# Causal attention scores from fp32 operands in 32-partition groups, two heads at a time

## The reference

```
q, k, v = (layernorm(x) Wq + bq), (ctx Wk + bk), (ctx Wv + bv)   # 4 batches x 16 heads of 16
QEr  = q . Er^T                                # (b, h, 512, 512)
Srel = skew(QEr)                               # row i shifted by its distance to the diagonal
attn = softmax(causal((q k^T + Srel) / 4)) v
x    = x + attn
x    = x + moe_ffn(layernorm(x));  x = x + cross_attention(layernorm(x));  x = x + ternary_ffn(x)
```

## Time and profile before

| | us |
|---|---|
| median of three runs | 1235.87 (1233.3 to 1241.53) |
| the profiled execution | 1240.44 |
| its span | 1238.3 |
| opening, up to the first `relative` | 0 to 86.6 |
| causal attention, to its last DVE instruction | 86.6 to 394.2 |

### The profile page before, as it was taken

How to read it: one execution, slowest core, us unless ns; L and a number is a source line. 1 busy time by engine, 2 the same in 40 slices (tenths; PEclk the granted TensorE clock), 3 DMA queues, 4 the chain that set the end, 5 groups by cost and what they waited for, 6 DMA issues and landing times. The chain is left out here.

```text
span 1238.3 us, 22330 instructions
## 1 busy us (share of the span) xinstructions
PE 1011.7 (82%) x6466; PEld 632.3 (51%) x6467; DVE 698.7 (56%) x2148; ACT 649.7 (52%) x1354; POOL 199.1 (16%) x466
## 2 busy tenths in 40 slices
PE   5746778877888769899999993538999999987487
PEld 3413455444454559898899993212333333334344
DVE  3844778888887541121111110866766666683697
ACT  1345767777773423222233331425777777763687
POOL 0000000000000012233222210002222222240232
PEclk9876999999999979899999997668999999998699
DMA  7478989999983845666666662463111111110001
GB/s 234 149 261 317 332 326 341 342 341 339 339 335 108 315 136 202 220 212 216 215 216 228 221 218 77 131 207 106 46 46 46 48 45 45 46 31 9 1 30 39
DMA packets 91721, 220.29 MB, mean 178 GB/s; under 512 B 8854, under 2 KB 52214, under 8 KB 85654
## 3 DMA queue, kind: packets, MB, share of 16 engines
q1 hardware_dynamic: 87926, 209.46, 49.2%
q0 software_dynamic: 3744, 10.23, 2.2%
HBM read 143.14 MB, written 76.41 MB: 177 GB/s over the span
## 5 line engine op out<-in xcount | busy, mean ns | idle before, releaser
L775 DVE CUSTOM_DVE_ANT_0 unused<-mpsS,mask_bias 128x512 bf16<-128x512 f32 x256 | 172.0, 691 | 84.0 <-PE mpsS L708 83.8
L1482 ACT ACTIVATE hT<-ph,w 128x128 f32<-128x128 f32 x312 | 89.0, 368 | 208.8 <-PE ph L1456 208.8
L802 ACT ACTIVATE mPT<-mpsB 128x512 f32<-128x512 f32 x256 | 152.6, 597 | 81.2 <-PE mpsB L715 74.8
L1456 PE MATMUL ph<-xT,w 128*128 128x128 f32 x1248 | 151.5, 281 | 8.8 <-DMA w<-in_w1p 8.1
L1501 DVE TENSOR_TENSOR xn<-py,b 128x256 f32<-128x256 f32 x39 | 16.5, 424 | 248.7 <-PE py L1466 248.7
L555 PE MATMUL psT<-ident,scores 128*128 128x128 f32 x640 | 108.0, 285 | 57.2 <-ACT scores L648 55.3
L1456 PEld LDWEIGHTS ph<-xT,w 128*128 128x128 f32 x1248 | 146.9, 197 | 11.9 <-issue 10.9
L603 DVE CUSTOM_DVE_ANT_0 scores<-psS,bias 128x512 f32<-128x512 f32 (+3 forms) x256 | 119.7, 487 | 47.8 <-DMA bias<-rel 21.8
L643 ACT COPY stage<-psE 128x512 f32<-128x512 f32 (+1 forms) x192 | 97.5, 510 | 93.6 <-DMA rel<-stage 58.1
L1466 PE MATMUL py<-w,hT 128*128 x624 | 141.2, 379 | 0.7 <-DVE xn L1501 0.7
L648 ACT ACTIVATE scores<-scores,nm 128x128 f32<-128x128 f32 (+3 forms) x256 | 136.6, 565 | 5.2 <-DVE nm L616 5.2
(11 more groups left out here) (258 smaller groups left out, 1435.8 us busy)
## 6 DMA issues: line engine op xcount, KB each, us to landing
rel<-stage SPq DMA_DIRECT2D x64, 640.0 KB, 6.6
bias<-rel SPq DMA_DIRECT2D x64, 640.0 KB, 7.2
w<-in_w1p SPq DMA_DIRECT2D x39, 1028.0 KB, 5.7
qk<-packed SPq DMA_DIRECT2D x64, 192.0 KB
mqk<-packed SPq DMA_DIRECT2D x64, 192.0 KB
w<-in_w2p SPq DMA_DIRECT2D x8, 1024.0 KB
b<-in_b SPq DMA_DIRECT2D x39, 128.0 KB, 6.1
got<-pair_out SPq DMA_DIRECT2D x8, 512.0 KB, 8.3
```

The costliest lines, as they stand in the source:

```text
L775: nc.vector.tensor_tensor_reduce(out=unused[:, i, :], in0=psS[i % 2][:, :], in1=mask_bias[:, i, :], scale=1.0, scalar=-3.0e38, op0=ALU.add ...
L802: nc.scalar.activation(PT[r][:, j, :], psB[j % 2][:, :], ACT.Exp, scale=1.0 / 4).then_inc(s_exp, 1)
L1456: mm = nc.tensor.matmul(ph[half][:, q * P:(q + 1) * P], w1[i][:, dk * F + f * P:dk * F + (f + 1) * P], xT[i][:, dk, :], start=(dk == 0), s ...
```

## The change

- `packed`, `qk`, `ErP` and the splitting go out of the first attention. Queries (`qf`, in the memory of `xn`) and keys (`kf`, in that of `xnT`) stay in SBUF as fp32, with `er` repeated over the partitions. The weights' rows are reordered on the host so that heads m of eight lie in four groups of 32 partitions: head m in group m mod 4, in its lower 16 partitions for m mod 8 < 4, in its upper 16 for the others. For an upper head the query comes from a copy in which the lower 16 rows are zeroed (`odd`), and all 32 rows are contracted.
- Heads go in pairs. `psE`, `psS`, `psT` are one pair of banks each, a bank for each head; ACT's stage copy, DVE's `PT` copy and the scaling of the maxima treat both heads in one instruction. One transfer of 1.28 MB writes `stage` for the pair, one reads `bias`.
- The stages are `REL` 5, `READ` 4, `SOFT` 2, `EXP` 1, now in pairs; there is no `LOAD`. PE's order in a unit is score of both heads, relative of both heads, the mask of both, then the transposes. All is written out, without the loop.
- `bias` has a third buffer in x's memory and zeroed queries are in ctxT's, so x and ctxT are read again at the end of the block.
- In the opening, LayerNorm goes batch by batch behind the values; ACT makes one copy of each product.

```
-            LOAD, REL, READ, SOFT, EXP = 8, 6, 4, 2, 1
+            REL, READ, SOFT, EXP = 5, 4, 2, 1
...
-                psE = banks(ctx, "psE", 2)
+                psE = ctx.enter_context(nc.psum_tensor("psE", [P, 2, 512], F32))   # psS, psT likewise
...
+                def where(p, h):
+                    m = 2 * p + h
+                    b, eh, odd, r = m // HEADS, m % HEADS // ROUND, m % ROUND // GROUP, m % GROUP
+                    return b, eh, odd, slice(ROWS * r, ROWS * r + (ROWS if odd else DH))
...
+                    def read(p):
+                        sp.wait_ge(s_wr[slot], 16 * (p // RING + 1))
+                        if p >= len(bias):
+                            sp.wait_ge(s_soft, 2 * NU * (p - len(bias) + 1))
+                        skewed = bass.AP(rel[slot].ap().tensor, P - 1, [[2 * REL_W - 1, P], [1, 2 * REL_W]])
...
+                    for n in range(-REL, NP - SOFT):
+                        if (p := pair_at(n, READ)) is not None:
+                            read(p)
+                        if (p := pair_at(n, REL)) is not None:
+                            write(p)
...
+                    def relative(p, u):
+                        wait(pe, s_eev, NU * p + u)
+                        for h in range(2):
+                            rows = where(p, h)[3]
+                            for i, off, w in units[u]:
+                                mm = nc.tensor.matmul(psE[:, h, off:off + w], query(p, h, i), er[rows, S - w:S],
+                                                      start=True, stop=True)
+                    def score(p, u):
+                        for h in range(2):
+                            wait(pe, s_soft, piece(p, u, h) - 1)
+                            for at, (i, off, w) in enumerate(units[u]):
+                                nc.tensor.matmul(psS[:, h, off:off + w], query(p, h, i), key(p, h, w),
+                                                 start=(at == 0), stop=False)
+                    def turn_probs(p, u):
+                        for h in range(2):
+                            if h == 0:
+                                wait(pe, s_tev, NU * p + u)
...
+                            if soft is not None:
+                                score(soft, u)
+                            if early is not None:
+                                relative(early, u)
+                            if soft is not None:
+                                hide(soft, u)
+                            if late is not None:
+                                turn_probs(late, u)
+                        g, half = divmod(n - 2, 2)
+                        if 0 <= g < NBH // GROUP:
+                            for j in (2 * half, 2 * half + 1):
+                                vals.weigh(pe, g, g % 2, j, s_tev, NU * 2 * (g + 1), ...)
+                        if n % 2 == 0 and 0 <= n // 2 - 2 < NBH // GROUP:
+                            vals.turn(pe, n // 2 - 2, 0)
...
+                                nc.vector.tensor_copy(PT[late % 4][:, :, 512 * u:512 * u + WU[u]],
+                                                      psT[:, :, 0:WU[u]]).then_inc(s_tev, 1)
```

More of the change, by code:

```diff
@@ L65, in build @@
     pair_out = dram("pair_out", (TOPK * TOK + SLOT_TILES * P, D), F32)
-    rel = [dram(f"rel_{r}", (P, REL_W), F32) for r in range(RING)]
+    rel = [dram(f"rel_{r}", (P, 2 * REL_W), F32) for r in range(RING)]
     with top:
@@ L243, in stored @@
                     sp.wait_ge(self.s_out[i], 3 * 16 * self.PARTS // self.depth)
[L245 to L281, removed]
         class ContextProjection:
@@ L500, in _, with query, key @@
+                def query(p, h, i):
+                    b, eh, odd, rows = where(p, h)
+                    if odd:
+                        return ctxT[rows, eh, b * S + i * P:b * S + (i + 1) * P]
+                    return qf[rows, b, eh, i * P:(i + 1) * P]
+                def key(p, h, w):
+                    b, eh, odd, rows = where(p, h)
+                    return kf[rows, eh, b * S:b * S + w]
                 @block.sync
                 def _(sp):
[L502 to L524, removed]
@@ new lines, in _ @@
+                    for i, name in enumerate(("L1_WkT", "L1_WvT")):
+                        sp.dma_start(wkv[:, i, :, :], a[name].rearrange("(k p) e -> p k e", p=P)).then_inc(s_wkv, 16)
+                    sp.wait_ge(s_soft, 2 * NU * NP)
+                    for half in range(2):
+                        part = slice(half * TOK // 2, (half + 1) * TOK // 2)
+                        sp.dma_start(ctxT[:, :, part], a["ctxT"].rearrange("(k p) t -> p k t", p=P)[:, :, part]).then_inc(s_back, 16)
+                    sp.dma_start(x[:, :, :], a["x"].rearrange("b (i p) d -> p (b i) d", p=P)).then_inc(s_back, 16)
@@ L527, in _ @@
+                    sp.wait_ge(s_wkv, 32)
+                    sp.wait_ge(s_back, 48)
                 @block.tensor
                 def _(pe):
[L529 to L534, removed]
-                        mm.then_inc(s_emm, 1)
@@ L537, in score @@
[L537 to L542, removed]
-                            mm = nc.tensor.matmul(psS[bank][:, off + w - P:off + w], identb[:, :], dmask[:, :],
-                                                  start=False, stop=True)
-                        mm.then_inc(s_smm, 1)
@@ L651, in step @@
+                                if i == 1:
                                     ex.then_inc(s_exp, 1)
[L652 removed]
         def masked_attention(mask_bias, maskT, identb, weights):
@@ L835, in _ @@
                     def _(sp):
-                        er_t = a["ErT"].tensor
-                        sp.dma_start(er[:, :], bass.AP(er_t, 0, [[0, PIECES], [S, DH], [1, S]])).then_inc(s_er, 16)
-                        k.load(sp)
-                        v.load(sp)
-                        for half in range(2):
-                            part = slice(half * TOK // 2, (half + 1) * TOK // 2)
-                            sp.dma_start(ctxT[:, :, part], a["ctxT"].rearrange("(k p) t -> p k t", p=P)[:, :, part]).then_inc(s_ctx[half], 16)
```

352 lines of the change are left out of this document (193 added, 159 removed).

## The result

The changed kernel takes 1271.9 us (1268.4 to 1276.7), the kernel before beside it on the same chip 1234.8 us: a ratio of 1.030, 95% interval 1.027 to 1.033. The forecast was 1229, a small gain; it came out on the other side. It lies within the range of 1195 to 1280, but by luck: the range was drawn that wide for rival B and the mild forms of rival C, and neither is what happened. The profiled execution took 1271.5 us, its span 1269.7.

The account below looks back on a forecast made before the run. It took transfers to bound the old block and a 9.1 us PE and DVE chain the new: 1240.44 + 17.4 (block) - 24.4 (opening) = 1233.4 us profiled, 1229 median; own range 1215 to 1243, wide range 1195 to 1280.

Parts of the forecast that it names:

- rival B: Block: the chain is shorter than summed, down to 8.2 us a pair, 27 us less, about 1202; chance 0.20.
- rival C: Score and relative: row groups don't overlap fully; mild forms about 1268, chance 0.22; others near 1334 or 1390, 0.04.
- part 1: Block: transfers bound the old one; without `qk` they take 7.7 us a pair, 1.3 less than the present step.
- Part 2: Score and relative: fp32 products on four row groups overlap fully, 2.14 us a pair; 8.5 us one after another.
- 3.07 times: Score and relative: skill's speedup for four row groups; would add 0.6 us a pair, some 19 us in all.
- strict program order: Score and relative: skill's rule that each head's second pass holds up the next head; near 1334 us.
- Part 4: Block: single-buffered PSUM makes a PE and DVE chain of 9.1 us a pair, against 9.0 before.
- rival D: SP's transfers form a ladder, each read waiting for the previous write: 9.4 to 11 us a pair, 1235 to 1275; chance 0.07.
- Part 5: Whole block: fill, 27 full steps and last steps sum to 325 us against 307.6, 17 us more.
- the two steps of scores without turns: Block, after the steps of relative alone: two steps without transposes, priced at 15 us.
- Part 6: Opening: first relative near 62 us instead of 86.6, 24.4 us gained.
- The reload: End of block: rereading x and ctxT, 12.3 us, costs nothing under 17 us of cover, up to 12 us without it.

Follow-up runs that it names:

- experiment 8: Kernel before the change with the scratch tensor `packed` laid out so a head's 96 rows stand at one step: 1223.2 us, ratio 0.9925.
- experiments 1 and 2: First: changed kernel with each step's write issued ahead of its read, 1244.1 us. Second: changed kernel without the writes of pairs 4 to 31, 1242.9 us.
- experiment 7: Three fills on the write-first kernel with weighing in the gaps: unit-matrix transposes (weighed heads' transposes also moved), 1218.4 us; two relative banks, 1208.1; both, fewer transposes, 1205.7.
- experiment 1: Changed kernel with SyncE issuing each step's write ahead of its read: 1244.1 us, ratio 1.0105.
- experiment 4: Weighing batches moved behind the turns of units 0 and 1: 1212.4 us on the changed kernel with write first, 1269.4 us on the changed kernel as is.

## Why the prediction was wrong, step by step

The marks of the block, from PE's timeline; "forecast" is the prediction's own sum laid out in time:

```
                                forecast  changed  write first
first relative at                  62       57.5      57.4
to first score (3 steps)           20       23.0      22.7
to pair 2 (2 steps)                15       21.5      21.4
to pair 29 (27 steps)             246      279.5     251.6
to the next block                  45       48.2      48.2
next block at                     388      429.7     401.3
```

**The bound before, part 1,** was right only in part: transfers did come late in the old block, but taking that lateness away gave 0.10 of 4.50 us a head (experiment 8). "So the block is bound by transfers" was read from a share of 0.91 and is not borne out. The sum does not rest on it, since it takes the old block as measured. In the kernels after the change the transfers take 0.73 to 0.88 of the DMA engines.

**Part 2, overlap: right**, rival C wrong. Four row groups run at once, not two by two, and not one after another. A round of four passes takes 0.53 us against 0.43 for one pass in a row, 3.2 times the speed of one after another and not four (an estimate from these rows); a unit of 512 columns still took the 1.07 us that the sum had for it, since the sum priced weights and layout beside the passes. That is near the 3.07 times of the Trainium skill that the prediction weighed, but no 0.6 us a pair came on top of the sum. The rule of the Trainium skill that I weighed there, strict program order, would have put the second pass of head 0 ahead of the first of head 1, if a product's two passes are issued one behind the other; the rows at 241.66 and 242.19 show otherwise, and here the measurement decides.

**Part 4, chain: right in size**, 9.1 against 9.32 measured once nothing else held the step (experiments 1 and 2). Over 27 steps that is 5.6 us. This held for the sum, not for the changed kernel itself, whose step was never the chain's once the ladder stood.

**What failed is the dismissal of rival D**, the step "at 9.1 us the write is issued when the read is already done". I gave D 0.07. It is false by the durations: a pair's write takes 4.5 us when alone and its read 5.6, and SyncE's order strings them together, read behind landed write and next write behind read. One after another they need 10.1 us, and the chain offers 9.3. So the read is not done when the next write is issued; the write lies behind it in the same queue and lands late, the next read is late by as much, and after some steps the write follows at 0.42 us. Then write and read always meet, the write takes 9.9 us, and the step is that plus the issue, 10.4 and more. The timeline above shows it happen: the writes of 111.46, 119.45 and 127.44 are only 8.0 us apart and catch up with the reads, and nothing later undoes it, since the ladder's rung is longer than the chain. My price for D, 9.4 to 11 us a pair, held: 10.66 a rung, and 28 us in all. What is shown is that the order of the two issues makes the ladder and that it stands once it has formed. The sum of 10.1 against 9.3 is an argument: the ladder formed over steps of 8.0 us, and no run shows whether steps of 8.6 and 10.0 by turns would have formed it alone, or that a step longer than 10.1 is free of it. Rows of before could have warned: a write of half the size took 6.7 us under load, and a read of half the size, in the same view,

```profile
bias<-rel SPq DMA_DIRECT2D x49, 640.0 KB, 7.2
```

By the Trainium skill, page "DMA: Bandwidth & Descriptors", section "Two DMAs through the same engine are not ordered", descriptors within one queue of one engine start in order. The trace agrees: the write takes 9.9 us behind the read, and 5.4 ahead of it.

**Part 5 was too low by 18 us even without the ladder:** the fill 3, the two steps of scores without turns 6.5 (priced at the full clock, while the changed kernel was granted 0.50 from 60 to 100 us; with the clock raised near 90 us they took 16.6 in place of 21.5, experiment 7), the chain's 5.6, the tail 3. **Part 6 was too high by 4.5.** The reload cost nothing, as said: PE waits 1.84 us at the next block where it waited 1.95. From there to the end the kernel is some 2.5 us shorter than before. So with these terms right and no ladder the profiled execution would have been forecast at 1233.4 + 18 - 4.5 - 2.5, near 1244, as experiment 1 has it: the small gain of the forecast was wrong even then. The change moves 192 KB a head less and frees 29 us of opening; the step of 9.3 us against 9.0, the longer fill with the slow clock in it, and the tail spend all of that.

**The ladder was only an order.** With the write first and the weighing in the gaps the same data path is 1.6% faster than before, with two banks in the fill 2.2 to 2.5%. Not tried: the reads on another queue, and transfers of one head each.

## What to carry to other kernels

When two dependent transfers of each step share one issuing queue, add their latencies and compare the sum with the step, and not only their bytes with the rate: here 4.5 + 5.6 us stood against 9.3, at a DMA share of only 0.73. Issue first the transfer that waits for an engine, and behind it the one that waits for a landing; an order that lets a write stand behind a read that waits for a write became a bound of its own here, which hides every gain elsewhere (32 us or nothing for the same edit). A high share of the DMA engines is no proof that they bind: take their lateness away and see what the step does (0.10 of 4.50 us here). And price a fill by the granted clock that its own rows show.

## What the runs showed of the hardware

- fp32 passes on four row groups run together: four of 512 columns start within 0.02 us of each other and the next four 0.53 us later, though the program calls one head's product after another. A unit took 1.07 us to its masks on four groups and 2.06 on two.
- A busy PE does not by itself get the full clock. With score and relative on the same two row groups it was busy for 59.66 of 60 us at 0.84; in the fill 24.00 of 24 us at 0.50, and with both score and relative under way 16.00 of 16 us still at 0.50. The same passes on four groups later ran 60 us at 1.00 with PE at 58.5 (experiment 4).
- Two transfers of 1280 KB in flight together take 5.4 and 8.5 us with the write first, 7.2 and 9.9 us with the read first.
- Laying `packed` out so that the 96 rows of `qk` stand at one step raised the DMA engines' share from 0.91 to 0.98, the rate only from 341 to 345 GB/s, and took ACT's wait for the writes from 45.9 us to 1.4 in 220.
